# First scan operands and last expert weights by matmul, constants on three queues, and own places for the two chunks at each end

## What is computed

```
x = layernorm(x + mamba(x))              # in-projection, 4-tap causal conv, silu, selective scan, out-projection
x = layernorm(x + retention(x, ctx))     # q from x, k and v from ctx, xPos rotation, decay mask, no softmax
x = layernorm(x + moe(x))                # 16 experts of width 64, top 2, plus a shared expert of width 128
```

```
proj  = xc @ W_xproj                     # 8 delta rows, then B (16) and C (16)
delta = softplus(proj[:8] @ W_dt + b_dt)
h     = exp(delta * A[s]) * h + delta * xc * B[s]     # over time, for each state s
y    += h * C[s]                                      # and + D * xc at the start
```

## Time and profile before

| | us |
|---|---|
| median of 3 runs | 1159.82 (1152.06 to 1161.8) |
| profiled execution, its own time | 1162.05 |
| its span, first to last instruction | 1160.2 |
| DVE busy / PE busy / ACT busy / POOL busy | 1064.0 / 1059.0 / 994.5 / 971.1 |
| first drive on DVE starts | 30.37 |

### The profile page before, as it was taken

One profiled execution on the slowest core, in us unless ns is written; L12 is line 12 of the kernel. 1 busy time (PEld: TensorE's weight loads), 2 busy tenths in 40 slices (PEclk: granted clock), 3 DMA queues, 4 the chain that ended last, 5 costly groups with the idle time before them and its releaser, 6 DMA issues. The chain is left out here.

```text
span 1160.2 us, 18257 instructions
## 1 busy us (share of the span) xinstructions
PE 1059.0 (91%) x5831; PEld 741.8 (64%) x5831; DVE 1064.0 (92%) x1492; ACT 994.5 (86%) x2176; POOL 971.1 (84%) x590
## 2 busy tenths in 40 slices
PE   5677888999999999999999989999999999899998
PEld 2455665666767666666666657666666667666665
DVE  2999999999999999999999979999999999999532
ACT  5888898999989898999989879898999989898443
POOL 0587788989989898898989869898989988898844
PEclk9787999999999999999999989999999999999899
DMA  6543543555565544555554364554555655444212
GB/s 165 209 175 138 178 172 130 174 188 190 182 205 178 178 154 156 187 212 192 185 180 145 135 186 179 183 186 163 169 175 186 211 192 166 168 154 157 82 69 74
DMA packets 84111, 194.49 MB, mean 168 GB/s; under 512 B 17288, under 2 KB 47936, under 8 KB 67632
## 3 DMA queue, kind: packets, MB, share of 16 engines
q1 hardware_dynamic: 84016, 193.33, 48.8%
HBM read 179.14 MB, written 5.77 MB: 159 GB/s over the span
## 5 line engine op out<-in xcount | busy, mean ns | idle before, releaser
L934 POOL TENSOR_TENSOR read<-state,bc_all 128x1024 f32<-128x1024 f32 x256 | 604.0, 2363 | 130.4 <-DVE state L804 109.6
L804 DVE TENSOR_TENSOR_SCAN state<-decay,drive_bank 128x512 f32<-128x512 f32 (+1 forms) x464 | 595.3, 1315 | 0.4
L754 ACT ACTIVATE decay<-delta,a_neg 128x252 f32<-128x252 f32 x1024 | 424.8, 494 | 0.9
L796 DVE TENSOR_TENSOR drive_bank<-dx_bank,bc_all 128x512 f32<-128x512 f32 (+1 forms) x496 | 328.4, 701 | 3.3 <-issue 2.3
L371 PE MATMUL y_bank<-ident,read 128*128 128x128 f32 x2048 | 279.2, 281 | 30.9 <-POOL read L934 30.8
L371 PEld LDWEIGHTS y_bank<-ident,read 128*128 128x128 f32 x2048 | 240.1, 145 | 101.6 <-POOL read L934 58.1
L973 POOL TENSOR_TENSOR hid<-gu,comb_all 128x512 f32<-128x512 f32 (+1 forms) x136 | 164.8, 1212 | 17.3 <-DVE gu L895 13.8
L362 PEld LDWEIGHTS down_bank<-down_w,hid 128*128 128x128 f32 x1024 | 129.4, 192 | 38.3 <-issue 30.0
L362 PE MATMUL bank<-x2T,gate_w 128*128 128x512 f32 (+1 forms) x272 | 139.0, 603 | 9.4 <-ACT delta L734 3.9
L362 PE MATMUL down_bank<-down_w,hid 128*128 128x128 f32 x1024 | 134.9, 277 | 2.6 <-POOL hid L973 0.7
L362 PE MATMUL bank<-x2T,up_w 128*128 128x512 f32 (+1 forms) x272 | 132.9, 582 | 0.8 <-ACT xc L710 0.7
(11 more groups left out here) (128 smaller groups left out, 1384.7 us busy)
## 6 DMA issues: line engine op xcount, KB each, us to landing
bc_all<-bc_dram SPq DMA_DIRECT2D x128, 1024.0 KB, 5.4
comb_all<-comb_dram SPq DMA_DIRECT2D x240, 128.0 KB, 3.0
x_in<-in_x_dram SPq DMA_DIRECT2D x15, 256.0 KB, 5.7
ctx_in<-in_ctx_dram SPq DMA_DIRECT2D x15, 256.0 KB, 6.3
k_pair<-k_pair SPq DMA_DIRECT2D x30, 128.0 KB, 2.1
q_pair<-q_pair SPq DMA_DIRECT2D x30, 128.0 KB, 2.5
out_dram<-y_out SPq DMA_DIRECT2D x15, 256.0 KB, 3.1
comb_all<-comb_dram SPq DMA_DIRECT2D x32, 64.0 KB, 2.6
```

The lines of the kernel that those rows point to most:

```text
L754: done = e.activation(seqs(decay_t[j % DECAYS][:, i, h, :])[:, :, 1:T], seqs(delta[c % 2][:, h, sub * SUB:(sub + 1) * SUB])[:, :, 1:T], AC ...
L796: e.tensor_tensor(drive_bank[:, a:b, :, :], dx_bank[:, :, :].unsqueeze(1).to_broadcast(shape), bc_all[group % BC_BUFS][:, 0, PAIR * i + a: ...
L804: e.tensor_tensor_scan(states(state_t[j % STATE_BUFS], a, b), states(decay_t[j % DECAYS], a, b), states(drive_bank, a, b), 0.0, ALU.mult, ...
L934: e.tensor_tensor(read_t[j % READS][:, :, :, :], state_t[j % STATE_BUFS][:, :, :, :], bc_all[group % BC_BUFS][:, 1, PAIR * i:PAIR * (i + 1 ...
```

## The change

Seven edits:

1. **First B and C by matmul.** For chunk 0's first four states, PE multiplies a one-column slice of `ident`, broadcast to 128 columns, with `proj` (eight products of 128x256) into `down_bank` and `y_bank`, and DVE copies the four results into `bc_all[0]` (`bc_copy`). The first DMA load of `bc_all` is gone.
2. **First `dx` on DVE**, straight into `dx_bank`; `proj` of chunk 0 is copied by DVE too.
3. **Last expert weights by matmul.** For chunk 16, PE multiplies a 0/1 `selector` with `combT` into the free PSUM tiles of the scan (eight products of 128x256), and DVE makes `hid` from them. The last `comb_store` and its 16 loads are gone.
4. **Constants on three queues.** ACT issues `ident`, `a_log`, `conv_w`, `conv_b`; POOL issues `w_out`, `down_w`; SP keeps the others, and issues those needed late at ticks -15, -7 and 1. The semaphores are finer.
5. **Function tables loaded ahead**: three tiny activations (`warm`) for Exp, Silu and Softplus in chunk 0; `a_exp` and `a_neg` are made first on ACT.
6. **Early centering** of `w_out` and `down_w`, behind `tap3` of chunk 0 (tick -23).
7. **`AT` gets five columns**: middle, last, second to last, first, second. The middle column keeps its places except `x_load`, which goes from -56 to -69. The `Exp` places get five lists as well.

In the order below: PE's first waits; the places; PE behind `dt_mm`; PE's weight products; the head of ACT; DVE's `dx` of chunk 0; the centering; DVE's `hid` of the last chunk.

```diff
-            w.wait_ge(S["first_consts"], 16 * 6)
+            w.wait_ge(S["ident"], 16)
+            w.wait_ge(S["tap_consts"], 16 * 2)
...
+COLUMN = [3, 4] + [0] * (CHUNKS - 4) + [2, 1]
+                place = SUB_TICKS * FIRST_SUB[c] + places[COLUMN[c]]
...
-    "x_load": [(-56, -88)],
+    "x_load": [(-69, -89, -61, -56, -67)],
-    "gate_z": [(10, 22), (40, 29)],
+    "gate_z": [(10, 24, 10, -22, 12), (40, 31, 40, 16, 40)],
-    "bc_store": [(-31, -27)],
+    "bc_store": [(-31, -25, -43, -22, -34)],
-    "ret": [(101, 90)],
+    "ret": [(101, 86, 99, 71, 99)],
+    "weight_mm": [
+        (-11, 122, -14, 18, -12), (-11, 123, -22, 18, 5), (-11, 123, -22, 4, -18), (-11, 123, -22, 7, -16),
+        (-11, 123, -22, -9, -12), (-20, 125, -8, 25, -8), (-11, 127, -14, 4, 5), (-2, 141, -15, 18, -12)],
-LAST_EXP_AT = [-10, -8, -3, 0, 3, 4, 16, 19]
+    [-9, -9, -4, -4, 1, 4, 5, 25],
...
                 for c in due(tick, "dt_mm"):
...
+                    if c == 0:
+                        for two in (0, 1):
+                            for pair in (0, 1):
+                                w.wait_ge(S["bc_copy"], 2 * two + pair - 1)
+                                for i in range(PAIR):
+                                    row = DT_RANK + GROUP * pair + PAIR * two + i
+                                    done = mm((down_bank, y_flat)[pair][:, i * SUB:(i + 1) * SUB],
+                                              ident[0:PROJ, row:row + 1].to_broadcast([PROJ, P]), proj[0:PROJ, 0:SUB])
+                                done.then_inc(S["bc_mm"], 1)
...
+                for c, pair in due(tick, "weight_mm"):
+                    w.wait_ge(S["combT"], at(c))
+                    w.wait_ge(S["state"], PAIR * STEPS)
+                    w.wait_ge(S["y_gated"], ALL_SUBS)
+                    w.wait_ge(S["selector"], 1)
+                    mm(last_weight(pair), selector[0:EXPERTS, pair * P:(pair + 1) * P],
+                       combT[:, 0:SUB]).then_inc(S["weight_mm"], 1)
...
+            e.dma_start(ident[:, :], io["c_ident"]).then_inc(S["ident"], 16)
...
+            per_channel(e, conv_b, io["L0_attn_conv_b"], S["conv_consts"])
+            w.wait_ge(S["zero"], DECAYS + 2)
+            warm(0, ACT.Exp)
...
+                for c, sub in due(tick, "dx"):
+                    bc_copy(0, 0)
+                    w.wait_ge(S["delta"], 2)
+                    w.wait_ge(S["xc"], HALVES)
+                    e.tensor_tensor(dx_bank[:, :, :], xc[0][:, :, 0:SUB], delta[0][:, :, 0:SUB],
+                                    ALU.mult).then_inc(S["first_dx"], 1)
+                    bc_copy(0, 1)
+                    bc_copy(1, 0)
+                    bc_copy(1, 1)
+                    w.wait_ge(S["d_consts"], 16 * 2)
+                    for h in range(HALVES):
+                        done = e.tensor_scalar(d_diag[:, h, :], ident[:, :], d_param[:, h:h + 1], 1.0, ALU.mult, ALU.mult)
...
-                        (0, -3, ((w_out[:, :, :], 0, HALVES), (down_w[:, :, :], HALVES, PAIRS))),
+                        (0, CENTER_TICK, ((w_out[:, :, :], 0, HALVES), (down_w[:, :, :], HALVES, PAIRS))),
...
+                    w.wait_ge(S["weight_mm"], pair + 1)
+                    w.wait_ge(S["down_mm"], at(c, index - 3, TILES))
+                    e.tensor_tensor(hid[index % 3][:, 0:SUB], gu[index % 2][:, 0:SUB], last_weight(pair),
+                                    ALU.mult).then_inc(S["last_hid"], 1)
```

More of the change, by code:

```diff
@@ L45 @@
 AT = {
[L46 to L82, removed]
@@ L101 @@
[L101 to L105, removed]
+    "xT_mm": [(-46, -46, -44, -59, -48)],
+    "tap_mm": [(-38, -37, -37, -48, -41)],
+    "xb_mm": [(-43, -42, -43, -55, -43)],
+    "proj_mm": [(-32, -23, -33, -26, -26)],
+    "dt_mm": [(-19, -19, -22, -13, -20)],
+    "ctxT_mm": [(62, 27, 60, 14, 55)],
+    "k_mm": [(69, 70, 69, 36, 67)],
+    "v_mm": [(68, 71, 62, 36, 62)],
@@ new lines @@
+    "out_mm": [(69, 70, 70, 38, 69)],
+    "q_mm": [(78, 72, 78, 51, 77)],
+    "r1_var_mm": [(86, 72, 86, 54, 86)],
+    "score_mm": [(94, 86, 94, 72, 94)],
+    "retout_mm": [(105, 91, 105, 76, 105)],
+    "x2T_mm": [(117, 97, 118, 92, 120)],
+    "router_mm": [(129, 101, 132, 94, 129)],
+    "combT_mm": [(136, 120, 136, 104, 135)],
+    "xT": [(-45, -45, -45, -52, -48)],
+    "conv_bias": [(-41, -41, -41, -47, -31)],
+    "proj": [(-24, -17, -27, -22, -23)],
+    "ctxT": [(59, 32, 57, 13, 55)],
@@ new lines @@
+    "v": [(66, 71, 61, 38, 66)],
+    "k_copy": [(67, 63, 65, 29, 64)],
+    "x1T": [(70, 68, 72, 38, 70)],
+    "q_copy": [(79, 72, 84, 45, 78)],
+    "r1_var": [(87, 72, 89, 63, 92)],
+    "ret_copy": [(100, 89, 104, 68, 98)],
+    "square2": [(108, 93, 106, 75, 108)],
+    "normed2": [(114, 99, 114, 81, 111)],
+    "x2T": [(118, 100, 116, 88, 116)],
+    "combT": [(137, 124, 136, 103, 136)],
+    "square3": [(189, 193, 189, 158, 188)],
+    "normed3": [(205, 193, 231, 164, 202)],
+    "xc0": [(-36, -35, -35, -39, -31)],
@@ new lines @@
+    "xc1": [(-33, -25, -33, -22, -29)],
+    "delta": [(-19, -16, -20, -21, -19)],
+    "top_tanh": [(130, 110, 130, 100, 130)],
+    "tap1": [(-39, -39, -38, -35, -30)],
+    "tap2": [(-37, -37, -36, -33, -29)],
+    "tap3": [(-36, -34, -35, -23, -25)],
+    "rstd2": [(111, 99, 103, 77, 111)],
+    "rstd3": [(196, 170, 205, 164, 197)],
+    "k_rot": [(74, 65, 70, 32, 80)],
+    "k": [(77, 82, 76, 40, 87)],
+    "q_rot": [(84, 70, 84, 55, 86)],
+    "q": [(87, 79, 88, 66, 90)],
+    "ret": [(101, 86, 99, 71, 99)],
@@ L258, in decoder_layer @@
             "score_mm", "ret_copy", "ret", "retout_mm", "x2T_mm", "x2T", "router_mm", "router", "top_tanh", "top_soft",
-            "comb", "combT_mm", "combT", "gate_mm", "up_mm", "silu", "gu", "hid", "down_mm")}
+            "comb", "combT_mm", "combT", "selector", "weight_mm", "last_hid", "gate_mm", "up_mm", "silu", "gu", "hid", "down_mm")}
         SQUARES, VAR_EPS, RSTD, NORMED = (
@@ L287, in blocks_of, with loads @@
             return width(c) // P
+        def loads(buffer, groups):
+            return uses(groups, buffer, BC_BUFS) - (1 if buffer == 0 else 0)
         def uses(before, buffer, buffers):
@@ L617, in _ @@
                     copy(xT[c % 3][:, 0:width(c)], bank_of["xT", c][:, 0:width(c)]).then_inc(S["xT"], 1)
+                    if c == 0:
+                        warm(1, ACT.Silu)
                 for c in due(tick, "conv_bias"):
+                    w.wait_ge(S["conv_consts"], 16 * 3)
                     w.wait_ge(S["xb_mm"], at(c))
@@ L781, in _ @@
                     for h in range(HALVES):
-                        e.tensor_scalar(d_diag[:, h, :], ident[:, :], d_param[:, h:h + 1], 1.0, ALU.mult, ALU.mult)
-                    w.wait_ge(S["a_exp"], 1)
-                    e.tensor_scalar(a_neg[:, :, :], a_exp[:, :, :], -1.0, 1.0, ALU.mult, ALU.mult).then_inc(
-                        S["mamba_dve"], 1)
+                        done = e.tensor_scalar(d_diag[:, h, :], ident[:, :], d_param[:, h:h + 1], 1.0, ALU.mult, ALU.mult)
+                    done.then_inc(S["d_diag"], 1)
```

263 lines of the change are left out of this document (165 added, 98 removed), and 4 rows, old and new, of the table EXP_AT.

## The result

| | before | after |
|---|---|---|
| median of 20 runs each | 1152.66 us (1145.78 to 1161.8) | 1161.15 us (1158.11 to 1169.16) |
| ratio | 1 | 1.0089, 95% interval 1.0071 to 1.0106 |
| profiled execution, its span | 1160.2 | 1157.1 |
| first drive starts | 30.37 | 22.20 |
| last scan ends | 1089.49 | 1084.02 |

The change costs 0.9% by the ratio, about 10 us (8.5 between the medians), where I forecast a gain of about 9. A trap stands in the first column: the profiled execution of before, 1162.05 us, was a slow one and lies just above the slowest of its 20 timed runs. Two single traces set side by side would say that the change gained 3 us. So from here on medians and ratios say how much, and traces say only where.

A forecast was written before the change was run, and what follows sets the result against it. DVE was taken to bound the middle and PE the end, after a start where DVE mostly waits. From 1162.05, -6.2 + 2.3 - 6.5 - 1.0 - 1.6 + 4.2 - 2.0 = -10.8 gave 1151 us, range 1143 to 1160.

The forecast's parts named there:

- the profiled execution as a base: The sum starts from the profiled 1162.05 us, taken as 2.2 above the median of three timed runs.
- first drive: At the start: the first drive comes at 24.2 us instead of 30.37, 6.2 us earlier, with bounds 21.0 and 26.4.
- taps inside the bound stretch: Start of the middle: chunk 1's three taps now fall where DVE is the bound, costing 2.3 us.
- x_load: Middle: loading x_in 13 ticks earlier removes PE's wait near 667 us and DVE's waits behind it, saving 6.5 us.
- waits ahead of the last scan, early y matmuls: Near the last scan: DVE's wait for late PE goes (-1.0), and step 255's y matmuls run earlier (-1.6).
- weight products and the waits in the end: End, bound by PE: eight weight products cost 4.2 us, while the five PE waits mostly go, saving 2.0.
- Net start: -3.9: Start: 6.2 us gained at the first drive less 2.3 us of chunk 1's taps leaves 3.9 us saved.
- one to one into the time: Middle: DVE is the bound, busy 394.79 of 400 us, so its work there counts fully in the time.
- My own mark for being wrong: Early scan: the forecast is wrong if DVE waits over 2 us between 25 and 60 us.
- The rival at 1163: Start: chunk 1 is as late as before, DVE waits at step 8, and all 3.9 us are given back; 1 in 10.
- Only `x_load` moves: Middle: the only place changed there is x_load, 13 ticks or about 11 us earlier.
- The first rival: Start and end: 1143 us, with fast first products (-2.8), weight products hidden in PE's wait (-4.2), fewer waits (-1); 1 in 6.

The follow-up runs named there:

- start_x: The kernel before with the start's edits, the places of chunks 0 and 1, and x_load at -69 for all middle chunks; old tail: 1151.56 us, ratio 0.9996.
- tail_only: The kernel before with the changed places of chunks 15 and 16 and the last expert weights by matmul, nothing else: 1164.89 us, ratio 1.0109.
- xload_only: The kernel before with x_load at -69 in place of -56 for all chunks but the first two and the last: 1145.87 us, ratio 0.9945.
- start_only: The kernel before with the start's edits and places of chunks 0 and 1; x_load at -56 except for chunk 2: 1166.53 us, ratio 1.0127.
- start_x_qswap: start_x with the store and reload of q for chunk 1 (q_swap) at 78 instead of 65: 1151.97 us, ratio 1.0002 to the kernel before.
- tail_x: The kernel before with x_load at -69, the changed places of chunks 15 and 16 and the last expert weights by matmul: 1158.26 us, ratio 1.0044.
- after_bcstore: The changed kernel with bc_store of chunk 15 turned back to -31 from -43: 1159.06 us, ratio 1.0057 to the kernel before.
- after_proj: The changed kernel with proj_mm of chunk 1 three ticks later, -23 for -26: 1161.05 us, ratio 1.0079 to the kernel before.
- after_rows128: The changed kernel with the last chunk's weight products over all 128 rows, zero-padded, in place of 16: 1158.73 us, ratio 1.0054 to the kernel before.
- tail_fixed: tail_x with bc_store of chunk 15 at -31 and the weight products over 128 rows: 1146.97 us, ratio 0.9966 to the kernel before.
- after_fixed: The changed kernel with bc_store of chunk 15 at -31, q_swap of chunk 1 at 78, weight products over 128 rows: 1153.92 us, ratio 1.0015 to before.

## Why the prediction was wrong

Point by point, with measured values against the terms of its sum. Medians of before are 1150.8 to 1152.7 in all comparisons.

| term | predicted | measured |
|---|---|---|
| the profiled execution as a base | 1162, "2.2 above the median" | 9.4 above the median of 20 |
| first drive | -6.2 | -8.2 |
| taps inside the bound stretch | +2.3 | +2.1 |
| waits behind the new start | 0 | about +12, as `start_x` adds 5.9 in all; in its trace 2.9 of it ahead of step 8, the rest behind |
| x_load | -6.5 | -6.3 |
| waits ahead of the last scan, early y matmuls | -2.6 | the y matmuls 1.0 earlier, the end no shorter |
| weight products and the waits in the end | +4.2 - 2.0 | between -1.3 and +1.5, with 128 rows |
| half clock behind 16-row products | not thought of | +1.7 to +5 |
| SP's wait for bc_store(15) | not thought of | +5 |
| steps 232 to 240, with the new places of the tail | 0 | +1.7 |

- **The base.** I took three runs as they were, one at 1152 and two near 1161, and read the stall in the middle as typical. With 20 runs the median is at 1152.66. The steps of the sum would have given about 1142 from there, so my 1151 was nearer to the outcome than my argument. The large stall's size, 6.5 us, is nonetheless what x_load alone is worth in the median. But it isn't in every execution: `tail_only` has the old start and the middle's x_load at -56 too, and in its trace PE waits for `x_in` once, for 0.5. With x_load at -69 no trace shows a wait for it behind 60 us. So the term was right, and its size in part by luck. DVE sat idle for 17.1 us between 200 and 940 in the profiled execution of before and for 4.4 in `xload_only`, so more than that one stall was untypical in it.
- **The first drive** came 2.0 earlier than I had it. The first products ran at 0.25 each and the others at 0.5 (my 0.44 was between), in all 5.6 us where I had 7.0, and the tap matmuls took 2.96 instead of 3.54. The wait for `tap_rows` went the other way: PE got it at 7.37 where I had 5.5, near my upper bound of 7.7. The centering ended at 14.04, 0.7 after proj_mm, and held DVE's copy of `proj`: PE waited 0.47 for it, so it was covered but for that.
- **The step that failed: that "Net start: -3.9" lasts.** What DVE does in the middle was to come "one to one into the time", and so the lead of the start was carried to the end, with no term for what DVE would wait for behind it. As far as step 8 the number held, by luck: step 8 came 4.4 us earlier, because the first drive came 2.0 earlier than I had it, and waits, the 2.47 at 40.21 above all, took 1.6 back. Then the lead goes. `start_x` begins step 8 at 3.6 us ahead of `xload_only`, step 40 at 1.7 behind and step 208 at 6.3 behind: 9.9 us in place of nothing.
- **Ahead of step 8** the wait at 40.21 has a cause that the rows show. Chunk 1's `xc` came at 33.73, for its taps now alternate with scans on DVE, and ACT has eight decays and a table load of 1.28 ahead of it. I named "what is queued behind" for the decays of step 2 and not for the y matmuls of steps 0 to 3, which stand behind chunk 1's proj_mm. My own mark for being wrong, a DVE wait over 2 us between 25 and 60, was met by it. The rival at 1163 has nearly the measured time, but not by what happened: `dx_bank` came at 54.1, ahead of its limit of 56 and of 57.9 before, and step 8 did not wait.
- **Between steps 8 and 40** seven of the eight kernels with the new start lose 4.6 to 6.4 us against `xload_only` (`start_only` more, by its x_load). In `start_x`, 4.7 of the 5.3 are idle time of DVE, 2.2 of them in steps 24 to 32. From step 40 to step 208 it is 0.1 to 4.6 us, another value in each trace; `start_x_qswap` loses 0.1 there and `start_x` 4.6. So only the first of the two is a steady cost of the new start; at step 40 the seven stand 1.7 to 3.0 us behind `xload_only`. In `start_x`, DVE is idle for 3.9 us between 24 and 60, 6.0 between 60 and 200 and 9.5 between 200 and 940; in `xload_only` it is 1.3, 2.4 and 4.4. That is 11.3 more.
- **"Only `x_load` moves" in the middle** was wrong in my reading of the table. The columns of the two chunks at an end lie on top of middle chunks: chunk 15's `bc_store` at tick 885 shares SP with chunk 12's loads. I had followed each moved DMA of the start past SP's queue and none of the tail. This is the second step that failed: SP's wait costs 5 us in the traces.
- **The products of the tail** were sized right: 16 instructions from 1133.40 to 1136.62 and from 1140.03 to 1140.80, 4.0 us. PE's waits between last scan and last matmul shrank from 2.5 to 1.3, 1.2 where I had 2.0. From last scan to last matmul the three kernels with 128 rows take 65.7 to 66.6 us, the five with the old end 65.1 to 67.0: at most +1.5, less than my +2.2. The clock I had taken as given. Behind 16 rows it cost an estimated 1.7 to 5 us, half of the 3.4 to 10.2 us at half clock.
- **Ahead of the last scan** PE no longer waits for `gate_z`, as forecast, but waits 1.33 for POOL at 1079.41 and 0.50 at 1081.87. The y matmuls of step 255 follow the last read at once, 3.0 us behind the last scan where it was 4.0, but the end is bound by PE's work and is no shorter for it.
- **The queues.** `tap_rows`, issued at 1.73, landed near 7.3, 5.6 us instead of the 2.8 of the earlier trace rows. Four other loads of 128 to 512 KB were on their way meanwhile. Before, it was issued at 2.67 and landed at 5.5: an issue 0.9 earlier, and a landing 1.8 later. The rule of the Trainium skill that I had weighed ("DMA: Bandwidth & Descriptors", Issuing engines are not separate DMA queues), that all queues share the same DMA engines, agrees with this. The load of a function table at 32.43 took 1.28, and `xc` began at 33.73. The drain of 1.38 that the Trainium skill adds to each switch ("ScalarE: Activation LUTs", What ACT_TABLE_LOAD costs) does not show here either.
- **Slips in the working**, none of which decides the outcome. With fast products the first drive is at 24.2 - 2.8 = 21.4 and not 21.0. Step 8 is reached at 59.9 - 3.9 = 56.0 and not 55.3. The first rival and a quarter of my own make 0.29 and not 0.34. A step in the middle takes 4.1 to 4.2 us and not 3.4, so 13 ticks are some 13 us.

**What stays open.** Why the rest of the lead goes between steps 8 and 40, and in some traces more of it from there on to 940. Three things come together up to step 40: new places of chunks 0 and 1, a lower clock from 100 to 150 us, and chunk 1's late chain. Two orders were tried on it, and neither gained. The new first drive with the old places of both chunks wasn't tried. Nor is it shown which of the tail's places costs the 1.7 us.

## What to carry to other kernels

A pipeline that starts earlier gains only what of the lead is left far behind the start. Follow it from hand-over to hand-over: here it was 8.6 us at the first scan, 3.6 at step 8 and gone before step 40, with 2.1 us of taps moved behind the start. Whether making the second chunk early too would have kept it was not tried. When a waiting DMA is moved ahead on an in-order queue, look for what other chunks have due in the same ticks, and not only at its own chunk. And before a sum is made against one profiled execution, find out where that execution lies among many runs: here it was 9 us from the median, as much as the whole effect.

## What the hardware showed that I had not expected

**Behind matmuls with few rows the clock of a busy PE fell.** In all five traces with 16-row weight products (after, `tail_only`, `tail_x`, `after_bcstore`, `after_proj`) the granted clock went to 1.2 GHz 2.6 to 3.8 us after the first such product, for 3.4 to 10.2 us, with PE busy without a gap. In all three with 128 rows (`after_rows128`, `tail_fixed`, `after_fixed`) it did not fall there. The products have the same columns and order and differ in nothing but rows that hold zeros. Besides that, `after_rows128` differs from after by one memset at the start. At the start, in every kernel with the 40-row products, the clock was at half from 17 to 20 us on for 6.8 us (3.4 in `start_only`); but two of the five traces with the old start (`tail_x`, `tail_fixed`) show such a slice too, which leaves that undecided.

**DVE's idle time goes with PE's time at half clock.** Between 200 and 940 us the 13 traces have between 6.8 and 27.3 us at half clock:

| half clock, us | 6.8 | 10.2 | 13.7 | 17.1 | 20.5 | 27.3 (before) |
|---|---|---|---|---|---|---|
| DVE idle, us | 4.4, 5.1, 5.1 | 6.0, 6.1, 6.1 | 7.9 | 8.5, 9.4, 9.5, 9.5 | 10.7 | 17.1, of it 6.5 behind x_in |

Without before, which has the stall behind x_in, about 0.4 us more of DVE's idle time stands beside each us that PE runs at half, though PE has slack there: in `xload_only` it is busy for 96% of that time. Which of the two comes first differs. The stretches of `start_x` around its first fall of the clock in this span, and around a later one:

```profile
298.00:301.40 3.40, 3.16 (x14) 1.67 (x14) 3.40 (x5) 3.37 (x12) 3.32 (x4) 1.00 0.73 292
301.40:304.80 3.40, 3.40 (x6) 1.50 (x6) 3.25 (x5) 3.21 (x7) 3.33 (x3) 0.53 0.49 161
304.80:311.60 6.80, 6.80 (x40) 4.79 (x39) 6.47 (x8) 4.67 (x9) 5.92 (x4) 0.98 0.78 310
...
519.90:523.30 3.40, 1.46 (x7) 0.72 (x7) 3.29 (x17) 3.38 (x13) 2.24 (x3) 1.00 0.42 171
523.30:526.70 3.40, 3.40 (x6) 1.33 (x5) 3.02 (x6) 2.36 (x7) 1.08 (x1) 0.52 0.20 77
526.70:533.50 6.80, 6.80 (x40) 4.88 (x38) 5.63 (x7) 4.80 (x10) 6.80 (x4) 0.99 0.19 46
```

At 301 DVE was full ahead of the fall and idle for 0.5 us in and behind it. At 523 PE had stood idle for 1.9 us of the stretch in front, and DVE was idle for 1.6 us in and behind it. So in some cases the lower clock comes before DVE's waits and in others a wait of PE comes before both; what DVE would have lost at full clock no run shows.
